# Row maxima of a two-pass attention: brought to their rows by TensorE and two copies, in place of a copy and two transfers

## The reference

```
x = layernorm(x + attn(x))            # 16 heads of 8, causal, softmax over 256 keys
x = layernorm(x + xattn(x, ctx))      # 16 heads of 8, 512 context keys + causal own keys
x = layernorm(x + ffn(x))             # s = x Win + bin; h = relu(s W1 + b1); g = h W2 + b2; out = g Wout + bout
softmax(d) = exp(d - max(d)) / sum(exp(d - max(d)))
```

## Time and profile before

| | us |
|---|---|
| three timed runs | 278.23, 279.88, 283.87 |
| their median | 279.88 |
| the profiled execution | 280.01 |
| its span, first to last instruction | 278.3 |

### The profile page before, as it was taken

How to read it: one execution, slowest core, us unless ns; L and a number is a source line. 1 busy time by engine, 2 the same in 40 slices (tenths; PEclk the granted TensorE clock), 3 DMA queues, 4 the chain that set the end, 5 groups by cost and what they waited for, 6 DMA issues and landing times. The chain is left out here.

```text
span 278.3 us, 7527 instructions
## 1 busy us (share of the span) xinstructions
PE 238.3 (86%) x2846; PEld 144.5 (52%) x2846; DVE 190.6 (69%) x415; ACT 165.5 (59%) x384; POOL 102.8 (37%) x282
## 2 busy tenths in 40 slices
PE   8797669798959998529999999999999999998681
PEld 5675536575844774204454653555455655544440
DVE  2949457884836879816998879987989689423331
ACT  3462235584831958116769777777977596974221
POOL 8214496771611429311214234222432142420311
PEclk9968689999797999957999999999999799998977
DMA  4649777099794006990700630000000000000000
GB/s 116 249 128 189 199 163 109 27 278 157 244 157 62 2 1 209 173 188 4 116 3 3 179 51 4 4 1 3 3 3 2 1 2 3 3 22 19 2 21 19
DMA packets 20933, 21.72 MB, mean 78 GB/s; under 512 B 1376, under 2 KB 18592, under 8 KB 20768
## 3 DMA queue, kind: packets, MB, share of 16 engines
q1 hardware_dynamic: 20464, 21.00, 34.2%
q10 hardware_dynamic: 432, 0.23, 0.4%
HBM read 11.85 MB, written 9.18 MB: 76 GB/s over the span
## 5 line engine op out<-in xcount | busy, mean ns | idle before, releaser
L871 ACT ACTIVATE probs<-psum 128x512 f32<-128x512 f32 (+1 forms) x256 | 118.0, 560 | 46.6 <-PE psum L1166 23.7
L980 DVE TENSOR_REDUCE pm<-psum 128x1 f32<-128x512 f32 x128 | 79.8, 681 | 21.6 <-PE psum L1146 21.1
L982 DVE TENSOR_REDUCE pm<-psum 128x3 f32<-128x384 f32 x128 | 63.3, 548 | 12.8 <-PE psum L1133 12.8
L1209 PE MATMUL psum<-probs,v 128*9 128x256 f32 (+5 forms) x1024 | 62.6, 368 | 1.6 <-POOL probs L807 0.9
L1166 PE MATMUL psum<-qk,km 51*128 51x256 bf16 x256 | 34.3, 277 | 8.8 <-DMA qk<-shift_rows 8.0
L1166 PE MATMUL psum<-qk 51*128 51x256 bf16 (+1 forms) x256 | 32.6, 260 | 9.4 <-DMA qk<-shift_rows 7.5
L1209 PEld LDWEIGHTS psum<-probs,v 128*9 128x9 f32 (+2 forms) x1024 | 25.0, 99 | 24.8 <-issue 7.2
L1146 PE MATMUL psum<-km,qk 48*128 48x512 bf16 x128 | 33.3, 393 | 4.0 <-DMA qk<-scr_qk 2.9
L807 POOL TENSOR_SCALAR_AFFINE_SELECT probs<-probs 128x512 f32<-128x512 f32 x32 | 20.0, 639 | 40.1 <-ACT probs L871 40.0
L1133 PE MATMUL psum<-neg,unit_b 64*128 64x256 bf16 (+1 forms) x256 | 34.1, 260 | 0.0
L1149 PE MATMUL psum<-qk 48*128 48x256 bf16 x128 | 28.9, 290 | 0.0
(11 more groups left out here) (114 smaller groups left out, 335.3 us busy)
## 6 DMA issues: line engine op xcount, KB each, us to landing
qk<-scr_qk SPq DMA_DIRECT2D x14, 384.0 KB, 6.9
km<-scr_m SPq DMA_DIRECT2D x8, 384.0 KB, 7.0
scr_qk<-spl SPq DMA_DIRECT2D x7, 384.0 KB, 3.4
scr_qk<-spl SPq DMA_DIRECT2D x21, 128.0 KB, 3.9
scr_m<-spl SPq DMA_DIRECT2D x4, 384.0 KB, 2.7
ctxT_sb<-ctxT SPq DMA_DIRECT2D x1, 1024.0 KB, 7.0
scr_m<-spl SPq DMA_DIRECT2D x4, 256.0 KB, 2.9
wb_sb<-wb SPq DMA_DIRECT2D x1, 642.0 KB, 5.0
```

The source lines that it names most:

```text
L871: nc.scalar.activation(probs[:, ring % PRING, r, 0:cols], bank_of(s)[:, 0:cols], ACT.Exp, scale=SCALE).then_inc(exp_done, 1)
L980: nc.vector.tensor_reduce(pm[:, place, 1 + 4 * qt:2 + 4 * qt], m, axis=AX.X, op=ALU.max).then_inc(reduced, 1)
L982: nc.vector.tensor_reduce(pm[:, place, 2:5], own_blocks(m), axis=AX.X, op=ALU.max).then_inc(reduced, 1)
L1209: last = nc.tensor.matmul(o, v[:, at:end], weights, start=(k == 0 and g in (0, NG - 1)), stop=(k == len(key_tiles(t)) - 1 and g >= NG - 2) ...
```

## The change

The three extra rows move from rows 48 to 50 of each half to rows 0 to 2, and the data to rows 3 to 50. `shift` is now eight matmuls of three columns of weights and 128 columns each (pair, head of the pair, query tile), whose output lies in partitions 0 to 2 (first heads) and 64 to 66 (second heads) of one bank, 512 columns wide. ScalarE copies the first heads' rows with scale -1 straight into `qk`, VectorE those of the second heads. `shift_rows`, `send_rows`, the 64 small transfers and their semaphores are gone; the first `T` tile of a step waits for the two copies.

Pass `S` now multiplies all 51 rows, so the three query rows have to be zero when it runs. VectorE writes zeros over the queries of units 1 to 3 before the plan, GpSimd over those of units 4 to 7 right after its split of them (`blanked`), and `take` of these units waits for it. In unit 0 `spread` gives zeros there.

`x_sb` and the biases are loaded at the start, behind the context. The planner's costs, `LATE`, and the steps after which GpSimd blanks `v2` and writes ones under `km` are changed, so that the order of the whole plan differs. The planner now models the transfers as one resource.

```diff
-VALUES_AFTER = (1, 3, 5)
-BLANK_AFTER = (2, 4, 6, 8)
+VALUES_AFTER = (4, 6, 8)
+BLANK_AFTER = (3, 5, 7, 9)
...
-LATE = [(("qk", 0), 0), (("qk", 1), 0), (("qk", 2), 1), (("v1", 0), 0), (("qk", 3), 3), (("v1", 1), 1), (("m", 0), 5),
-        (("vm", 0), 11), (("m", 1), 6), (("vm", 1), 13), (("m", 2), 12), (("vm", 2), 15), (("m", 3), 22),
-        (("vm", 3), 25)]
+LATE = [(("qk", 0), 0), (("qk", 1), 0), (("qk", 2), 3), (("v1", 0), 0), (("qk", 3), 5), (("v1", 1), 1), (("m", 0), 0),
+        (("vm", 0), 15), (("m", 1), 7), (("vm", 1), 14), (("m", 2), 13), (("vm", 2), 11), (("m", 3), 25),
+        (("vm", 3), 21)]
...
-        "window": 0, "borrow": 400, "gap": 500, "fill": 115, "filled": 0.6, "pv_soon": 300, "pv_few": 2,
-        "pv_left": 4, "pv_hold": 0, "p_misc": 0.0, "p_late": 2.2, "p_mlp": 4.0, "p_behind": 3.5, "p_pv": 2.2,
-        "p_pv_on": 0.0, "p_row": 1.5, "p_switch": 0}
+        "load": 90, "window": 80, "borrow": 400, "gap": 500, "fill": 115, "filled": 0.6, "pv_soon": 300, "pv_few": 1,
+        "pv_left": 2, "pv_hold": 0, "p_misc": 0.0, "p_late": 4.0, "p_mlp": 4.0, "p_behind": 1.0, "p_pv": 2.2,
+        "p_pv_on": 3.5, "p_row": 1.5, "p_switch": 1.2}
...
-        shift_rows = sb("shift_rows", [PARTS * HG, ROWBUFS, T], BF16)
...
-        def send_rows(engine, t):
-
-            g = group(t)
-            for r in range(2):
-                rows = PARTS * 2
-                dst = qk[HALF * r + DATA:HALF * r + ROWS, unit(t) % B, 2 * g:2 * g + 2, 0, :]
-                engine.dma_start(dst, shift_rows[rows * r:rows * (r + 1), t % ROWBUFS, :]).then_inc(rows_in[g], 16)
+        def zeros_under(engine, queries):
+
+            return engine.memset(queries.bitcast(F32), 0.0)
...
+            sp.dma_start(x_sb[:, :, :], x_rows.rearrange("(n p) c -> p n c", p=P)).then_inc(x_in, 16)
+            sp.dma_start(bias_sb[:, :], biases.to_broadcast([P, 2 * C])).then_inc(bias_in, 16)
...
                         nc.gpsimd.tensor_sub(low[1], rest[:, T:], mid[:, 1, :]).then_inc(split_done[i], 1)
+
+                        zeros_under(nc.gpsimd, qk[:, s[1] % B, :, 0, :]).then_inc(blanked, 1)
...
-                        if t >= ROWBUFS:
-                            act.wait_ge(rows_in[group(t - ROWBUFS)], rows_landed(t - ROWBUFS))
-                        last = nc.scalar.activation(shift_rows[:, t % ROWBUFS, :], m[0:PARTS * HG, 0:T], ACT.Copy, scale=-1.0)
+                        rows = half(qk[:, unit(t) % B, 2 * group(t):2 * group(t) + 2, 0, :], 0, PARTS)
+                        last = nc.scalar.activation(rows, half(m, 0, PARTS).rearrange("k (a t) -> k a t", a=2), ACT.Copy, scale=-1.0)
...
             for u in range(1, B):
                 ones_under(nc.vector, qk[:, u, :, 1, :]).then_inc(qk_ones, 1)
+                zeros_under(nc.vector, qk[:, u, :, 0, :]).then_inc(qk_ones, 1)
...
+                elif what == "shift":
+                    t = s[1]
+                    sem_, value = misc_ready(s)
+                    dve.wait_ge(sem_, value)
+                    rows = half(qk[:, unit(t) % B, 2 * group(t):2 * group(t) + 2, 0, :], 1, PARTS)
+                    maxima_of = half(bank_of(s), 1, PARTS).rearrange("k (a t) -> k a t", a=2)
+                    nc.vector.tensor_scalar_mul(rows, maxima_of, -1.0).then_inc(second_in, 1)
...
-                        pe.wait_ge(rows_in[group(t)], rows_landed(t))
+                        wait_misc(("shift", t))
...
-                queries, keys = (half(qk[:, u % B, p, a, :], r, DATA) for a in range(2))
+                queries, keys = (half(qk[:, u % B, p, a, :], r, ROWS) for a in range(2))
...
                         for qt in range(QT):
-                            parts = max_s[:, t % ROWBUFS, qt].rearrange("p r k a -> p (r k a)")
-                            last = nc.tensor.matmul(m[0:PARTS * HG, qt * P:(qt + 1) * P], parts, ident_b[:, :], start=True,
-                                                    stop=True)
+                            for a in range(2):
+                                for r in range(2):
+                                    last = nc.tensor.matmul(half(m, r, PARTS)[:, a * T + qt * P:a * T + (qt + 1) * P],
+                                                            max_s[:, t % ROWBUFS, qt, r, :, a], ident_b[:, :], start=True, stop=True)
```

More of the change, by code:

```diff
@@ L314, in emit @@
             end = run_pe(s, r, PE_COST[what]) + COST["lat"]
-            if what == "shift":
+            if what == "shift" and in_place(n):
+                end = max(run("act", end, ACT_COST["maxima"]), run("dve", end, DVE_COST["maxima"]))
+                done[("rows", n)] = end + 60
+            elif what == "shift":
                 end = run("act", end, ACT_COST[what])
@@ L573, in decoder_layer @@
         ln_no = numbered(norms)
+        shift_no = numbered(s for s in plan if s[0] == "shift")
         order_of = {k: numbered(s for s in plan if s[0] == k) for k in ("ln1", "wo", "mo")}
@@ L646, in half, with data @@
             return tile[HALF * r:HALF * r + rows]
+        def data(tile, r):
+            return tile[HALF * r + PARTS:HALF * r + ROWS]
         def wb1(name):
@@ L897, in _ @@
                     last.then_inc({"ln1": x1_ready, "wo": x2_ready, "mo": x3_ready}[kind_], 1)
-                elif what == "rows" and rows_on_act(s[1]):
-                    sem_, value = emptied(("shift", s[1]))
-                    act.wait_ge(sem_, value)
-                    send_rows(act, s[1])
                 elif s in act_no:
```

69 lines of the change are left out of this document (30 added, 39 removed).

## The result

The kernel after the change takes 287.47 us (median of 4 runs, 286.98 to 291.33), the kernel before took 279.06 beside it (278.17 to 283.87). The ratio is 1.031 [1.026, 1.036]: the change makes the kernel 3.1% slower. Forecast were 272 us, at most 281. The profiled execution took 287.69 with a span of 286.0, against a span of 278.3 before. In all that follows a median and its range are of all runs of a kernel, a ratio only of those within some 1.5% of its fastest, so that the two can disagree by a few us where a kernel scatters.

A forecast was written before the change was run, and what follows sets the result against it. TensorE was taken as the bound from 140 to 240 us, with waits for small transfers the larger part of its idle time before. 280.0 - 20.6 + 4.2 + 3.5 + 2 + 3 = 272.1, say 272 us, range 264 to 281.

The forecast's parts named there:

- removal of the transfers: TensorE's four waits for the maxima's small transfers go, 15.5 us, with 5.1 of lower clock behind them: 20.6 us saved.
- Would other waits take it?: Whether other waits replace the removed ones: not for the 8.03 us wait; for the first, a margin of a few us.
- the clock's 5.1 us: Lower TensorE clock after the long waits, priced window by window as 2.4, 0.4, 0.6 and 1.7 us, all regained.
- 3.2 us, and I add 1.0 (0 to 2) for a lower clock: At the start, VectorE's zeros over three units' queries delay unit 0's split; with the lower clock 4.2 us added.
- I take 3.5: TensorE's eight shift matmuls in place of two, run two at a time over 32 steps: 3.5 us, ends 0 and 10.6.
- rival E: Weight loads and matmuls of shift follow one another, 27.3 us in all, total 296 us; chance 0.05.
- It fits: VectorE's new copy, 22.0 us over 32 steps, fits its idle time at 93% busy; cost 2 us (0 to 8).
- VectorE above 90% in the full stretch: Sign expected in the changed profile: VectorE over 90% busy in the full stretch, 140 to 240 us.
- Rival D: VectorE becomes the bound, its 22.0 us of copies fall on the path in full, total 289 us; chance 0.08.
- GpSimd's four memsets: zero: GpSimd's zeros run while put is under way and only take waits: no cost; 3.6 us without that cover.
- The new order can't be costed by row. I take 3 (0 to 8): Work pulled forward in the new plan meets takes that aren't, causing new waits: 3 us, 0 to 8.
- Rival B: Next data late: the first half's three waits, 7.4 us, return for takes of units 1 to 4; 279.5 us, chance 0.2.

The follow-up runs named there:

- b_norows: Kernel before without the 64 small transfers of the maxima (three query rows stay zero, exponential's scale 0.001): 264.16 us, ratio 0.951.
- a_old: Kernel after, with its new data path, walked in the order of the kernel before: 283.39 us, ratio 1.016.
- a_old_zeros: a_old with the zeros of units 1 to 3 written by GpSimd in place of VectorE: 279.12 us, ratio 0.996.
- b_pe: Kernel before with four times the matmuls of shift, in two column groups in turn: 282.69 us, ratio 1.015.
- b_dve: Kernel before with one more VectorE instruction per step, a maximum over 128x512 in SBUF that nobody waits for: 286.07 us, ratio 1.017.
- b_norows_work: b_norows with the extra VectorE instruction of b_dve and the extra matmuls of b_pe: 273.72 us, ratio 0.975.
- b_norows_work2: b_norows_work with GpSimd's four memsets of zeros behind its splits of units 4 to 7: 276.54 us, ratio 0.992.
- a_old_zdve: a_old_zeros with the zeros of units 4 to 7 written by VectorE behind its part of the split, not GpSimd: 278.66 us, ratio 0.998.
- a_zeros_ones: Kernel after with zeros of units 1 to 3 and ones under batch entry 0's context keys written early by GpSimd: 277.43 us, ratio 0.988.

## Why the prediction was wrong

Two steps failed above all. The gain was taken at 20.6 us and measured at 13.7 (15.9 by the medians). And the work added in every step and unit was taken at 5.5 us (3.5 + 2 + 0) and measured at 11.4, for the most part because GpSimd's zeros stood in the sum at nothing. The long wait that the order brought was not foreseen, though the 3 us taken for the order nearly cover what the order costs in sum. The terms beside what the runs showed, a ratio's difference times 280 us:

```
term                                 forecast   runs
removal of the transfers              -20.6    -13.7 [-16.4, -11.0]   b_norows
zeros at the start, VectorE            +4.2     +5.6 [2.9, 8.3]       a_old, a_old_zeros
eight matmuls                          +3.5     +4.2 [1.7, 6.7]  \    b_pe
VectorE's copy                         +2       +4.8 [2.9, 6.8]  /    b_dve; together +6.7 [2.0, 11.4], b_norows_work
GpSimd's zeros                          0       +4.7 [0.5, 8.9]       b_norows_work2 (2.8 by medians)
new order                              +3       +4.4 [1.8, 7.1]       a_old
sum on 280.0                           272.1    287.7                 after, by its ratio: 288.8
```

The last line proves less than it seems to. Most terms are differences between neighbours in one row of kernels (`b_norows`, `b_norows_work`, `b_norows_work2`; `a_old_zeros`, `a_old`, after), so they must add up along each row. The one free check is where the two rows meet: `b_norows_work2`, which is before without the transfers and with stand-ins for the new work, is at 0.992, and `a_old_zeros`, the real new path, at 0.996. That is 1.1 us apart, with an interval of -1.0 to 3.2. So the stand-ins cover the new path, while the prices inside them, with intervals of 2 to 5 us to either side, are rough.

**"Would other waits take it?"** Right for the 8.03 us wait, as the timeline argued: 11.6 us became 4.6. The step that failed is the size of the removal, on two points. Of 15.5 us of waits about 12.6 became work. And the clock's 5.1 us were counted whole. In `b_norows` the last two of the four terms come (1.00 from 110 to 140 us), of the 2.8 us counted for 30 to 40 about half: 4.00 x 0.34 = 1.4 of loss is left there. What that gives is taken back elsewhere in the first stretch, whose mean stays at 0.87. A clock term counted window by window assumes that nothing else lowers the clock nearby.

**"3.2 us, and I add 1.0 (0 to 2) for a lower clock."** The 3.2 were 3.0. The clock term was mis-sized: `rep` took 3.2 us longer, not 1.0. Its own row had 2.8 us after a wait of 4.04, above the upper bound of 2 that it set for a wait of 4.5. What stands behind the wait is `rep`, 4.3 us of unbroken work at full clock: `a_old`, idle for 4.47 us, has it at 7.79. The busy time right behind the wait is the bound to use.

**"I take 3.5" and the weights.** Near enough: 4.2 [1.7, 6.7]. Eight matmuls take 0.39 us at full clock, and their eight weight loads, 85 ns each, 0.20 us together; rival E is refuted. The Trainium skill, "TensorE: Matmul & The Clock Gate", The mechanism, names two cases in which a load is pulled ahead: another row group, or the background weight buffer. The prediction cited only the first. The trace shows that loads of full-row weights overlap, which the first doesn't allow; whether it is by that buffer, no run shows.

**"It fits"** (VectorE, 2 with bounds 0 to 8). Inside the bounds, half the size. 93% busy was right for `b_dve`, where nothing waits for the extra instruction and it cost 22% of its time; but the stretch that is 93% busy had 1.6 us of that. The forecast for the kernel after, VectorE above 90% in the full stretch, was wrong: it is 85.31 of 100, with TensorE busy 95.04 there for 97.48. Rival D, 22 us in full, is refuted.

**"GpSimd's four memsets: zero."** Wrong. The cover named, `put` under way, covers only `take`. What stands behind the memsets on GpSimd itself, `rstd` and the mask, was not looked at, though the earlier trace rows has TensorE waiting 0.86 us for that mask already. The bound given for no cover, 3.6 us, was the right size. The price is rough, 4.7 us [0.5, 8.9], and `a_old_zdve` didn't win it back.

**"The new order can't be costed by row. I take 3 (0 to 8)."** The number is near (4.4), and wrong in its make-up: 11.1 us lost to one wait (6.8 once the start is mended), and the rest of the order gains 2 [0, 4.3] (`a_zeros_ones` 0.988, `a_old_zeros` 0.996). That the sum came near is luck. The wait was readable in the diff: `LATE` of `m` 0 goes from 5 to 0, `BLANK_AFTER` from 2 to 3, and `take` waits for `km_ones` ahead of the next `put` in SyncE's queue. The prediction looked for slow transfers ("work pulled forward will meet takes that aren't") and did not walk the queue. Rival B, takes of units 1 to 4 late by 7.4 us, comes nearest: the wait was 7.8, for unit 2. Its cause was another, an issue held up and not full transfers (the share was 0.00 in 34 to 39 us), and it came with a low clock on top, 2.9 us.

**The sum as a whole.** All five costs were too small, by 0.7 to 4.7 us, and the gain too large by 5 to 7: a sum of one large gain and five small costs, four of them taken in the lower part of their own bounds, was no centre. The range ended at 281 though the bounds named in the text (2, 8, 3.6, 8, 10.6) reached much further.

## What to carry to other kernels

When a change moves a transfer's issue, write out the queue that issues it, with what each entry waits for and when that is made: an entry needed late that waits for something late, in front of one needed now, costs the whole wait and then the clock. Price added work where the waits are, not only where its engine is busiest: here most of it fell between steps 15 and 19. A cost hidden by a wait is not free if the same change removes the wait: price it in the kernel without the wait. For zeros or ones written ahead of time ask who stands behind them on the engine that writes them, not only who waits for them.

## What the runs showed of the hardware

The start: how long 48 matmuls last goes with TensorE's idle time right before them, 4.15 us after none, 4.34 after 1.25, 5.41 after 1.97, 6.14 after 2.31 and 7.79 after 4.47; in after they last 7.58, at a granted clock of 0.50 in 20 to 25 us. The wait of 7.8 us in the middle has about 2.9 us of low clock behind it: 0.50 and then 0.70 in the ten microseconds from 55 us, after a window in which TensorE did nothing. VectorE's cast from f32 to bf16 (128x512) takes 0.43 us alone and 1.15 and 1.49 where it begins beside a row of GpSimd's memsets, ending just behind the last of them. And 32 instructions of 0.675 us on VectorE that nobody waits for cost 4.8 us, 1.6 of it in the stretch in which they bring VectorE to 93%.
